# Causal attention inside a four-layer kernel: TensorE makes the products with the values, and the sums of a first half, for two rounds at a time

## The chip, the core and the metric

One NeuronCore of one Trainium2 chip runs the whole program in one launch. The metric is the device time of one execution in microseconds (us). The engines are TensorE (PE, with PEld for its weight loads), VectorE (DVE), ScalarE (ACT), GpSimd (POOL) and SyncE (SP), which here only issues DMAs. Each has its own instruction stream and runs it in order; between streams there are semaphores.

## The reference

Four layers run one after the other, each with a residual and layer norms around it: a convolution model, a feed-forward layer, this attention, and a feed-forward layer with mixed LoRA experts. The change touches the attention alone:

```python
b, t, d = x.shape                       # 2, 1024, 1024; H, G, HD = 32, 8, 32
q = jnp.dot(x, Wq).reshape(b, t, H, HD).transpose(0, 2, 1, 3)
kv = jnp.dot(x, Wkv).reshape(b, t, G, 2, HD).transpose(2, 3, 0, 1, 4)
k, v = (kv[:, 0], kv[:, 1])             # each of the 8 groups is shared by 4 heads
scores = jnp.einsum('bhqd,bhkd->bhqk', q, k)
scores = jnp.where(causal[None, None], -jnp.inf, scores)
weights = jax.nn.softmax(scores * (1.0 / HD ** 0.5), axis=-1)
ctx = jnp.einsum('bhqk,bhkd->bhqd', weights, v)
ctx = ctx.transpose(0, 2, 1, 3).reshape(b, t, d)
return jnp.dot(ctx, Wo) + bo
```

## The kernel before, in words

The program has four stages with a barrier between them. Stage C (`StageC`, lines 1466 to 2222) is the attention; its main loop runs from about 1083 us to 1915 us of the profiled execution.

**Groups.** The loop goes over 16 groups o: two batch entries times eight key groups, each with its four heads g. A group has 48 slots s, and S = 48 o + s counts slots through the whole loop. Slot s is round r = s // 4 of head g = s % 4. A round is one tile of 128 keys against one half (512) of the queries (`ROUNDS`, line 1428): rounds 0 to 3 are the first half, with 512, 384, 256 and 128 queries left by the causal rule, rounds 4 to 11 the second half, with 512 queries in rounds 4 to 8 and then 384, 256 and 128. R = 12 o + r counts rounds through the loop.

**TensorE, per slot** (`pe`, line 1886). It makes the scores of this slot, 128 keys by up to 512 queries (`pe_score`, line 1840), into one of three PSUM banks, which it may reuse once ScalarE has taken the exponential of the slot three before. Then it makes a product for the row maxima of a later group, 60 slots ahead (`pe_amax`, line 1824), into a bank that VectorE must have read (the maxima are taken at lines 2134 and 2138). In slots named by the table `JOBS` it also makes three matmuls of 512 columns of a coming group's queries or keys (`pe_job`, lines 1800 to 1802); 16 such steps are a job of two parts, and `evac_at`, `split_at` and `place_at` say at which slots the results are copied out, the next weights are split into a high and a low part in four pieces, and the results are moved by DMA.

**The products with the values.** Once per round, in its second slot (g == 1), TensorE makes the products of round R - 2 (`pe_pv`, line 1855): four heads, each into its own 32 partitions of bank 5, in the tile shape 128 x 32. The four heads are eight matmul records. In rounds 0 to 3 (and in all of group 15) four more with a matrix of ones follow (`pe_sums`, line 1873), which give the softmax sums of that half. Only after these does the semaphore `pv_s` count the round.

**ScalarE, per slot** (`act`, line 2022). The exponential of the slot goes to the buffer P (`act_exp`, line 2002). P holds three rounds, so the first exponential of round R waits until the products of round R - 3 are counted by `pv_s`; those of the second half also wait for GpSimd's additions from three rounds before. Between the exponentials, in the order of its stream, ScalarE copies out the jobs (line 1966), makes the high parts of the weight pieces (line 1942; in eight groups at slots 18 to 21, behind the exponential of the same slot), and copies out sums and products (lines 2015 and 2020) at slots 6 and 22.

**The sums of the second half.** VectorE adds the exponentials of rounds 4 and 5, one head per slot, after the row maxima of slots 24 to 27 (`dve_pair`, line 2104). GpSimd adds rounds 6 to 11 to that, one after the other (`pool`, line 2219), with the causal masking of the rounds on the diagonal in between (line 2207). In slot 5 of the next group TensorE reduces the result with ones (`pe_sum`, line 1882). GpSimd also multiplies a finished half by its reciprocal sums (line 2197) in rounds 1 and 5.

**Banks.** `tables` (line 1516) plays through the order of the loop and gives each use of three shared banks (3, 4, 6) its bank; the sums of a first half take one at slot 9 and give it back at slot 21.

After group 13 the weights of the next stage (`WO`, line 1463) are loaded and split in pieces too (ScalarE line 1948, VectorE line 2095), at slots of groups 13 to 15; SP issues the next load, and behind it the DMA of the row maxima of the next group, only when VectorE has made the four pieces before.

Of the kernel before, what the change touches and what calls it, by code (L numbers as in the profile page):

```python
# [235 lines left out]
class StageA:  # L236
# [332 lines left out]
    def pe(self, e):  # L569
        e.wait_ge(*self.k.cst_in(2))  # L570
        for name, *at in self.order["pe"]:
            if name[:2] == "b_":
                self.then.first_pe(e, name, *at)
            elif name == "tr":
                self.pe_tr(e, *at)
            elif name == "win":
                self.pe_win(e, *at)
            elif name == "out":
                self.pe_out(e, *at)
            else:  # L580
                self.pe_step(e, name, *at)
# [884 lines left out]
class StageC:  # L1466
# [49 lines left out]
    def tables(self):  # L1516


        self.step_at, self.evac_at, self.place_at, self.split_at = {}, {}, {}, {}
        for n, (what, slots, place) in enumerate(JOBS):  # L1520
            if slots:
                for q, S in enumerate(slots):
                    self.step_at[S] = (n, q)
                self.evac_at[slots[7] + 1], self.evac_at[slots[15] + 1] = (n, 0), (n, 1)
                self.place_at[place[0]], self.place_at[place[1]] = (n, 0), (n, 1)

                soon = n + 1 < len(JOBS) and JOBS[n + 1][1][0] < slots[15] + 8
                for q in range(4):
                    self.split_at.setdefault(slots[15] + 2 + q // (2 if soon else 1), []).append((n + 1, q))
        self.bank_of, self.held_by = {}, {}  # L1530
        given, keeps = [None] * 3, []

        def turn(o, a):
            b = keeps.pop(0)
            self.bank_of[o, a], self.held_by[o, a] = (3, 4, 6)[b], given[b]
            given[b] = o, a
            return b

        keeps += range(3)
        for o, a in [(0, a) for a in range(48)] + [(0, 48)] + [(1, a) for a in range(LEAD)]:  # L1540
            keeps.append(turn(o, a))
        for o in range(16):
            for s in range(48):
                A = 48 * o + s + 48 + LEAD
                if A < 768:
                    keeps.append(turn(A // 48, A % 48))
                if s == 38 and o < 15:
                    keeps.append(turn(o + 1, 48))
                if s == 5 and o > 0:
                    keeps.append(turn(o, 50))  # L1550
                if s == 9:
                    kept = turn(o, 49)
                if s == 21:
                    keeps.append(kept)
        turn(16, 50)
# [330 lines left out]
    def pe(self, e):  # L1886
        for u in range(18):
            if u < 16:
                self.pe_x(e, u)
            if u > 1:  # L1890
                self.pe_v(e, u - 2)
            if u in (10, 11):
                for q in range(8):
                    self.pe_job(e, 0, 8 * (u - 10) + q)
        for n in (1, 2):
            for q in range(16):
                self.pe_job(e, n, q)
        ahead = [(0, a) for a in range(48)] + [(1, a) for a in range(LEAD)]
        for q in range(32):
            self.pe_job(e, 3 + q // 16, q % 16)  # L1900
            for o, a in ahead[max(0, 5 * (q - 8) // 2):max(0, 5 * (q - 7) // 2)]:
                self.pe_amax(e, o, a)
                if a == 47:
                    self.pe_mrow(e, 0)
        for o in range(16):
            for s, (r, g) in enumerate(SLOTS):
                S = 48 * o + s
                self.pe_score(e, o, r, g)
                A = S + 48 + LEAD
                if A < 768:  # L1910
                    self.pe_amax(e, A // 48, A % 48)
                if s == 38 and o < 15:
                    self.pe_mrow(e, o + 1)
                if S in self.step_at:
                    self.pe_job(e, *self.step_at[S])
                if g == 1 and S > 8:
                    self.pe_pv(e, *divmod(S // 4 - 2, 12))
                if s == 5 and o > 0:
                    self.pe_sum(e, o - 1)
        self.pe_pv(e, 15, 10)  # L1920
        self.pe_pv(e, 15, 11)
# [223 lines left out]
    def dve(self, e):  # L2145
        k = self.k
        for u in range(16):
            self.dve_x(e, u)
            if u == 0:
                self.dve_w(e, 0)  # L2150
                self.dve_w(e, 1)
                e.memset(self.maskw[:, 0:384], 0.0).then_inc(self.given_s.s, 1)
            if u in (6, 12):
                self.dve_w(e, 2 if u == 6 else 3)
            if u in (12, 13):
                self.dve_job(e, 0, u - 12)
        e.wait_ge(*self.vmm_s(16))
        e.memset(self.K4[96:97, 0:8:2, :].bitcast(F32), -1.0).then_inc(self.given_s.s, 1)
        e.memset(self.K4[96:97, 1:8:2, :].bitcast(F32), -1.0).then_inc(self.given_s.s, 1)
        e.wait_ge(*self.given_s(3))  # L2160
        for n in (1, 2):
            for part in range(2):
                self.dve_job(e, n, part)
            self.dve_w(e, n + 3)
        ahead = [(0, a) for a in range(48)] + [(1, a) for a in range(LEAD)]
        for q in range(32):
            for o, a in ahead[max(0, 5 * (q - 8) // 2):max(0, 5 * (q - 7) // 2)]:
                self.dve_amax(e, o, a)
            if q % 8 == 7:
                self.dve_job(e, 3 + q // 16, q % 16 // 8)  # L2170
            if q == 15:
                self.dve_w(e, 6)
        for o in range(16):
            for s in range(48):
                S = 48 * o + s
                A = S + 48 + LEAD
                if A < 768:
                    self.dve_amax(e, A // 48, A % 48)
                if S in self.evac_at:
                    self.dve_job(e, *self.evac_at[S])  # L2180
                if 24 <= s < 28 and o < 15:
                    self.dve_pair(e, o, s - 24)
                for n, q in self.split_at.get(S, ()):
                    self.dve_w4(e, n + 1, q)
                for q in range(4):
                    if S - q in WO:
                        self.dve_wo(e, WO.index(S - q), q)
                E = self.finish_at(S, 2)
                if E is not None:
                    self.dve_rec(e, E)  # L2190
        self.dve_rec(e, 31)
# [491 lines left out]
```

## Time and profile before

| | |
|---|---|
| median of 3 runs | 2441.47 us (2439.51 to 2441.91) |
| the profiled execution | 2444.48 us |
| its span, first to last instruction | 2442.8 us |
| busy in the span: PE, DVE, ACT, POOL | 89%, 60%, 38%, 36% |
| mean granted TensorE clock | 0.946 of full speed |

Busy time counts instructions that overlap once, and the end of a matmul is modelled, so a busy TensorE is not one at its peak. The span is shorter than the time of its own execution by 1.68 us. In a row of the time line stand the start (us from the start of the span), the duration, engine, line, operation, the tiles written and read, their shape, how often it is repeated in the row, and in brackets the idle time of the engine before it and what ended that.

### The profile page before, as it was taken

Reading aid. Unit: us, or ns where it says so; the run is one execution under the profiler, and the core shown is the slowest. Engines: PE = TensorE matmul, PEld = TensorE weight load, DVE = VectorE, ACT = ScalarE, POOL = GpSimd, SP = SyncE. Lnnn points to the kernel's source line nnn. Section 1 sums busy time; section 2 is a strip of 40 time slices with the busy share of each in tenths; the row PEclk is TensorE's granted clock in tenths of the full one; section 3 lists DMA queues with packets and bytes.
Section 4 is the critical chain, followed back from the end, with each engine's and each line's share of the span. In section 5 each row is a group of like instructions: output and inputs, shape, how many; then the busy total and the mean of one; then the engine's idle time right before and its main releaser. Section 6 shows DMA issues by size and latency. Waiting matters only on the chain.

```text
span 2442.8 us, 31296 instructions
## 1 busy us (share of the span) xinstructions
PE 2167.2 (89%) x11064; PEld 1530.1 (63%) x11064; DVE 1459.2 (60%) x3261; ACT 924.3 (38%) x1691; POOL 889.7 (36%) x732
## 2 busy tenths in 40 slices
PE   4899965699999969789998899899987699999998
PEld 4655534588888859655555555555543387667676
DVE  7866766577766643277666566676675156543333
ACT  4654633233323223115554455355555222221111
POOL 1344654444444420004664454446654122110000
PEclk9899987899999989889999899999988899999999
DMA  5220445111211227431223622322222555334332
GB/s 164 72 90 1 149 130 193 64 69 71 77 70 70 87 93 267 109 75 45 67 61 85 187 71 68 73 75 67 52 68 65 173 174 172 133 115 158 112 112 95
DMA packets 139572, 249.30 MB, mean 102 GB/s; under 512 B 26885, under 2 KB 69765, under 8 KB 139191
## 3 DMA queue, kind: packets, MB, share of 16 engines
q1 hardware_dynamic: 130711, 230.51, 29.7%
q10 hardware_dynamic: 8704, 16.78, 2.1%
q8 instruction: 88, 1.44, 0.3%
q14 instruction: 69, 0.57, 0.1%
HBM read 139.48 MB, written 76.02 MB: 88 GB/s over the span
## 4 chain that ended last, share of the span: by engine, by line
PE 61%; DVE 11%; POOL 11%; issue 6%; DMA 3%; ACT 3%; SPq 3%; POOLq 0%; DVEq 0%; ACTq 0%
POOL c_S L2219 9%; PE PS L2403 4%; PE PS L2360 4%; PE PS L2361 4%; PE PS L2364 4%; PE PS L1069 3%; PE PS L1070 3%; PE PS L1071 3%; PE PS L1840 3%; PE PS L1824 3%; PE PS L1855 3%; PE PS L1102 2%; DVE PS L2138 2%; PE PS L1800 2%; PE PS L1104 2%
## 5 line engine op out<-in xcount | busy, mean ns | idle before, releaser
L2002 ACT ACTIVATE c_P<-PS 128x512 f32<-128x512 f32 (+3 forms) x768 | 360.6, 495 | 378.4 <-PE PS L1840 359.7
L2219 POOL TENSOR_TENSOR c_S<-c_S,c_P 128x2048 f32<-128x2048 f32 (+1 forms) x90 | 313.7, 3485 | 74.4 <-DVE c_S L2104 67.2
L1824 PE MATMUL PS<-c_K,c_Q 96*128 96x512 f32 (+3 forms) x768 | 283.3, 379 | 54.3 <-DVE cst L2138 27.2
L1840 PE MATMUL PS<-c_Q,c_K 97*128 97x512 f32 (+3 forms) x768 | 283.1, 381 | 9.2 <-DMA c_Q<-c_mT 5.6
L1840 PEld LDWEIGHTS PS<-c_Q,c_K 97*128 97x128 f32 x768 | 149.3, 197 | 169.5 <-ACT c_P L2002 74.1
L2134 DVE TENSOR_REDUCE cst<-PS 128x1 f32<-128x512 f32 x256 | 176.1, 688 | 97.3 <-PE PS L1824 97.0
L1824 PEld LDWEIGHTS PS<-c_K,c_Q 96*128 96x128 f32 x768 | 151.7, 198 | 124.6 <-DVE cst L2138 61.7
L2207 POOL TENSOR_SCALAR_AFFINE_SELECT c_P<-c_P 128x512 f32<-128x512 f32 x128 | 82.4, 644 | 373.1 <-ACT c_P L2002 373.1
L1855 PE MATMUL PS<-c_P,c_V 128*32 128x512 f32 (+3 forms) x1536 | 172.0, 521 | 19.0 <-ACT c_P L2002 11.3
L2138 DVE CUSTOM_DVE_ANT_0 PS<-PS,maskw 128x128 f32<-128x128 f32 (+3 forms) x256 | 126.8, 507 | 87.5 <-PE PS L1824 87.3
L2360 PE MATMUL PS<-c_xth,d_xh 128*128 128x512 f32 x384 | 157.2, 409 | 19.1 <-DVE d_xl L2475 19.1
L2138 DVE CUSTOM_DVE_ANT_0 PS<-PS,maskw,cst 128x128 f32<-128x128 f32 (+3 forms) x256 | 142.4, 556 | 46.9 <-PE PS L1824 31.6
L199 POOL TENSOR_TENSOR maskw<-maskw,mhalf 128x1 f32<-128x1 f32 x64 | 36.6, 572 | 360.3 <-DVE maskw L168 360.3
L1069 PE MATMUL PS<-b_w13h,b_xsh 128*128 128x460 f32 (+1 forms) x384 | 148.3, 386 | 16.6 <-DVE b_xsl L1274 16.3
L1301 DVE SCALAR_TENSOR_TENSOR b_pr<-b_g,b_a 128x460 f32<-128x460 f32 x192 | 158.3, 860 | 1.6
L1193 ACT ACTIVATE b_g<-PS 128x460 f32<-128x460 f32 x96 | 53.0, 554 | 267.5 <-PE PS L1076 267.5
L2361 PE MATMUL PS<-c_xtl,d_xh 128*128 128x512 f32 x384 | 152.4, 397 | 0.0
L1395 POOL TENSOR_TENSOR b_gp<-b_g 128x230 f32<-128x230 f32 x96 | 84.8, 883 | 165.3 <-DVE b_g L1286 165.3
L1070 PE MATMUL PS<-b_w13l,b_xsh 128*128 128x460 f32 (+1 forms) x384 | 143.9, 375 | 0.0
L1071 PE MATMUL PS<-b_w13h,b_xsl 128*128 128x460 f32 (+1 forms) x384 | 143.0, 372 | 0.0
L1800 PE MATMUL PS<-c_xth,c_wh 128*128 128x512 f32 x304 | 126.5, 416 | 8.3 <-DVE c_ql L2123 5.1
L1286 DVE TENSOR_TENSOR b_g<-b_g,PS 128x460 f32<-128x460 f32 x96 | 60.4, 629 | 119.2 <-ACT b_g L1193 119.2
(280 smaller groups left out, 4876.0 us busy)
## 6 DMA issues: line engine op xcount, KB each, us to landing
a_xin<-in_x SPq DMA_DIRECT2D x32, 512.0 KB, 4.3
c_Q<-c_qh SPq DMA_DIRECT2D x256, 64.0 KB, 2.0
d_x<-scr SPq DMA_DIRECT2D x32, 512.0 KB, 3.9
scr<-a_xin SPq DMA_DIRECT2D x16, 512.0 KB, 5.5
scr<-a_hid SPq DMA_DIRECT2D x16, 512.0 KB, 2.9
b_xn<-scr SPq DMA_DIRECT2D x16, 512.0 KB, 5.6
b_x<-scr SPq DMA_DIRECT2D x16, 512.0 KB, 4.8
scr<-b_x SPq DMA_DIRECT2D x16, 512.0 KB, 2.6
```

The costliest lines, as they stand in the source:

```text
L1069: e.matmul(o, self.xsh[:, par, i, :], wh[:, v, i, :], start=i == 0, stop=False)
L1070: e.matmul(o, self.xsh[:, par, i, :], wl[:, v, i, :], start=False, stop=False)
L1071: e.matmul(o, self.xsl[:, par, i, :], wh[:, v, i, :], start=False, stop=False)
L1824: e.matmul(bank[:, 0:hi - lo], self.Q4[0:96, 4 * (o % 3) + g, 128 * t:128 * t + 128], self.K4[0:96, HEADS[o % 8], lo:hi], start=True, stop ...
L1840: e.matmul(self.k.bank(i % 3)[:, 0:hi - lo], self.K4[0:97, HEADS[o % 8], 128 * kt:128 * kt + 128], self.Q4[0:97, 4 * (o % 3) + g, lo:hi], ...
L1855: m = e.matmul(k.bank(5)[32 * g:32 * g + 32, lo - 512 * half:512], self.V[:, kt, o // 8, HEADS[o % 8], :], P[:, g, 0:hi - lo], start=kt == ...
L2002: e.activation(self.P[:, R % 3, g, 0:hi - lo], self.k.bank(i % 3)[:, 0:hi - lo], ACT.Exp, scale=SCALE).then_inc(self.exp_s.s, 1)
L2134: e.tensor_reduce(m, r, AX, ALU.max).then_inc(self.mx_s.s, 1)
L2138: e.tensor_tensor_reduce(out=r, in0=r, in1=self.maskw[:, 512 - n:512], scale=1.0, scalar=m if lo > 0 else -3.0e38, op0=ADD, op1=ALU.max, a ...
L2219: e.tensor_tensor(S[:, :, 512 - n:512], S[:, :, 512 - n:512], P[:, :, 0:n], ADD).then_inc(self.psum_s.s, 1)
L2360: e.matmul(o, h, wh[:, c, cols], start=c == 0, stop=False)
L2361: e.matmul(o, h, wl[:, c, cols], start=False, stop=False)
```

## The change

TensorE makes the products with the values only in every second round, in slots 5, 13, 21, 29, 37 and 45, and there for the two rounds R - 3 and R - 2. The bank of a first half's sums is therefore taken at slot 13 and no longer at slot 9. VectorE's four additions of rounds 4 and 5 move one slot later.

```diff
@@ tables
-                if s == 9:
+                if s == 13:
                     kept = turn(o, 49)
@@ pe
-                if g == 1 and S > 8:
-                    self.pe_pv(e, *divmod(S // 4 - 2, 12))
+                if s % 8 == 5 and S > 8:
+                    for R in (S // 4 - 3, S // 4 - 2):
+                        self.pe_pv(e, *divmod(R, 12))
                 if s == 5 and o > 0:
                     self.pe_sum(e, o - 1)
@@ dve
-                if 24 <= s < 28 and o < 15:
-                    self.dve_pair(e, o, s - 24)
+                if 25 <= s < 29 and o < 15:
+                    self.dve_pair(e, o, s - 25)
```

TensorE, group 12, from the products at slot 17 to the end of those at slot 21. L1840 is a slot's scores, L1824 the product for the maxima, L1855 the products with the values, L1873 the sums. Before:

```order
L1855 MATMUL PS<-c_P,c_V 32x256 x4
L1873 MATMUL PS<-c_P,cst 32x256 x4
L1840 MATMUL PS<-c_Q,c_K 128x512
L1824 MATMUL PS<-c_K,c_Q 128x512
L1840 MATMUL PS<-c_Q,c_K 128x512
L1824 MATMUL PS<-c_K,c_Q 128x256
L1840 MATMUL PS<-c_Q,c_K 128x512
L1824 MATMUL PS<-c_K,c_Q 128x512
L1840 MATMUL PS<-c_Q,c_K 128x512
L1824 MATMUL PS<-c_K,c_Q 128x384
L1855 MATMUL PS<-c_P,c_V 32x128 x4
L1873 MATMUL PS<-c_P,cst 32x128 x4
```

Now, TensorE from slot 18 to the end of the products at slot 21:

```order
L1840 MATMUL PS<-c_Q,c_K 128x512
L1824 MATMUL PS<-c_K,c_Q 128x512
L1840 MATMUL PS<-c_Q,c_K 128x512
L1824 MATMUL PS<-c_K,c_Q 128x256
L1840 MATMUL PS<-c_Q,c_K 128x512
L1824 MATMUL PS<-c_K,c_Q 128x512
L1840 MATMUL PS<-c_Q,c_K 128x512
L1824 MATMUL PS<-c_K,c_Q 128x384
L1855 MATMUL PS<-c_P,c_V 32x256 x4
L1873 MATMUL PS<-c_P,cst 32x256 x4
L1855 MATMUL PS<-c_P,c_V 32x128 x4
L1873 MATMUL PS<-c_P,cst 32x128 x4
```

The products and sums of round 2 (256 columns) moved from slot 17 to slot 21, behind the scores of slots 18 to 21 and in front of those of round 3.

VectorE, group 12, from the maxima of slot 24. `ISA` at L2138 are the masked maxima with their accumulator read, L2104 is the addition of rounds 4 and 5. Before:

```order
L2138 ISA PS,cst<-PS,maskw 128x128
L2138 ISA cst 128x1
L2104 TENSOR_TENSOR c_S<-c_P 128x512
L2138 ISA PS,cst<-PS,maskw 128x256
L2138 ISA cst 128x1
L2104 TENSOR_TENSOR c_S<-c_P 128x512
L2138 ISA PS,cst<-PS,maskw 128x384
L2138 ISA cst 128x1
L2104 TENSOR_TENSOR c_S<-c_P 128x512
L2138 ISA PS,cst<-PS,maskw 128x512
L2138 ISA cst 128x1
L2104 TENSOR_TENSOR c_S<-c_P 128x512
```

Now, from the maxima of slot 25 (every line of this function is one further down):

```order
L2139 ISA PS,cst<-PS,maskw 128x256
L2139 ISA cst 128x1
L2105 TENSOR_TENSOR c_S<-c_P 128x512
L2139 ISA PS,cst<-PS,maskw 128x384
L2139 ISA cst 128x1
L2105 TENSOR_TENSOR c_S<-c_P 128x512
L2139 ISA PS,cst<-PS,maskw 128x512
L2139 ISA cst 128x1
L2105 TENSOR_TENSOR c_S<-c_P 128x512
L2135 TENSOR_REDUCE cst<-PS 128x1
L2105 TENSOR_TENSOR c_S<-c_P 128x512
```

The fourth addition now stands behind one more instruction, the maxima of slot 28 (TENSOR_REDUCE). The streams of ScalarE, GpSimd and SP are as they were.

## Rows read from the trace of the kernel before

**Rows 1.** The page: busy time in the span by engine, share and instructions.

```profile
PE 2167.2 (89%) x11064; PEld 1530.1 (63%) x11064; DVE 1459.2 (60%) x3261; ACT 924.3 (38%) x1691; POOL 889.7 (36%) x732
```

**Rows 2.** Time line, POOL, group 12: multiplication in round 5, additions of rounds 6, 7.

```profile
1741.26 1.27 POOL L2197 TENSOR_TENSOR c_cH<-c_cH,c_cS 128x512 f32<-128x512 f32 x1 [7.56 <-ACT c_P L2002]
1746.46 9.32 POOL L2219 TENSOR_TENSOR c_S<-c_S,c_P 128x2048 f32<-128x2048 f32 x2 [3.93 <-DVE c_S L2104]
```

**Rows 3.** Time line, PE: reductions at slot 5 (groups 5, 12, 13), a wait before.

```profile
1350.93 1.04 PE L1882 MATMUL PS<-c_S,cst 128*32 128x512 f32 x8
...
1721.25 1.07 PE L1882 MATMUL PS<-c_S,cst 128*32 128x512 f32 x8 [0.22 <-POOL c_S L2219]
...
1765.91 0.64 PE L1855 MATMUL PS<-c_P,c_V 128*32 128x256 f32 x8 [1.01 <-ACT c_P L2002]
...
1770.25 1.06 PE L1882 MATMUL PS<-c_S,cst 128*32 128x512 f32 x8 [0.23 <-POOL c_S L2219]
```

**Rows 4.** Time line, PE: products at slot 33 of group 12 and what follows.

```profile
1749.07 1.07 PE L1855 MATMUL PS<-c_P,c_V 128*32 128x512 f32 x8
1750.06 0.50 PE L1840 MATMUL PS<-c_Q,c_K 97*128 97x512 f32 x1
1750.40 0.39 PE L1824 MATMUL PS<-c_K,c_Q 96*128 96x512 f32 x1
1750.64 0.39 PE L1800 MATMUL PS<-c_xth,c_wh 128*128 128x512 f32 x1
```

**Rows 5.** Time line, PE: products and sums at slots 17 and 21 of group 12.

```profile
1734.35 0.64 PE L1855 MATMUL PS<-c_P,c_V 128*32 128x256 f32 x8
1734.80 0.61 PE L1873 MATMUL PS<-c_P,cst 128*32 128x256 f32 x8
...
1737.75 0.45 PE L1824 MATMUL PS<-c_K,c_Q 96*128 96x384 f32 x1 [0.16 <-DVE cst L2138]
1738.13 0.43 PE L1855 MATMUL PS<-c_P,c_V 128*32 128x128 f32 x8
```

**Rows 6.** Time line, ACT, group 12: weight piece of slot 19, exponential of slot 20.

```profile
1737.17 0.41 ACT L1942 CAST c_wh<-c_raw 128x256 fp32r<-128x256 f32 x1
1737.46 0.61 ACT L2002 ACTIVATE c_P<-PS 128x512 f32<-128x512 f32 x1
```

**Rows 7.** Time line, DVE, group 12: low parts, first and last addition of rounds 4, 5.

```profile
1735.50 0.69 DVE L2123 TENSOR_TENSOR c_ql<-PS,c_qh 128x512 fp32r<-128x512 f32 x1 [0.63 <-ACT c_qh L1966]
...
1738.55 0.42 DVE L2090 TENSOR_TENSOR c_wl<-c_raw,c_wh 128x256 fp32r<-128x256 f32 x1
...
1741.51 1.57 DVE L2104 TENSOR_TENSOR c_S<-c_P 128x512 f32<-128x512 f32 x1
1743.00 0.42 DVE L2138 CUSTOM_DVE_ANT_0 PS<-PS,maskw 128x256 f32<-128x256 f32 x1
...
1745.63 0.68 DVE L2104 TENSOR_TENSOR c_S<-c_P 128x512 f32<-128x512 f32 x1
```

**Rows 8.** Time line, DVE, group 14: pieces of slots 27 and 28, maxima between.

```profile
1846.50 0.41 DVE L2095 TENSOR_TENSOR c_xtl<-c_raw,c_xth 128x256 fp32r<-128x256 f32 x1
1846.83 0.68 DVE L2134 TENSOR_REDUCE cst<-PS 128x1 f32<-128x512 f32 x1
1847.43 4.13 DVE L2095 TENSOR_TENSOR c_xtl<-c_raw,c_xth 128x256 fp32r<-128x256 f32 x1
```

**Rows 9.** Time line, PE: waits at slot 41 of group 13, slot 0 of group 15.

```profile
1805.06 1.93 PE L1855 MATMUL PS<-c_P,c_V 128*32 128x512 f32 x8 [2.17 <-POOL c_P L2207]
...
1871.08 1.22 PE L1840 MATMUL PS<-c_Q,c_K 97*128 97x512 f32 x2 [5.57 <-DMA c_Q<-c_mT]
```

**Rows 10.** Time line, PE, group 15: from one round's products to the next.

```profile
1897.76 1.06 PE L1855 MATMUL PS<-c_P,c_V 128*32 128x512 f32 x8
...
1899.61 0.96 PE L1840 MATMUL PS<-c_Q,c_K 97*128 97x512 f32 x3
...
1901.22 1.07 PE L1855 MATMUL PS<-c_P,c_V 128*32 128x512 f32 x8
```

## The prediction

> **What bounds the kernel now.** I read the page first: TensorE is busy for 89% of the span [rows 1]. That alone would make it the bound, so the next question is what TensorE waits for in the attention loop. The time line of its reduction at slot 5 answers that. From group 12 to group 13 these lie 1770.25 - 1721.25 = 49.0 us apart, and each is preceded by a wait that GpSimd's last addition ends [rows 3]. I found the same mark, with the same 49.0 us where two such groups follow each other, in ten of the fifteen reductions. Where it is missing (the reduction at 1350.93 has no wait [rows 3]) the groups carry denser jobs, or are the last ones.
>
> So ten groups run in a closed loop of two halves. The first: VectorE ends the fourth addition of rounds 4 and 5, GpSimd starts its own at 1746.46 [rows 2] and TensorE reduces their sum at 1770.25, 23.8 us later. The second: from the reduction at 1721.25 to GpSimd's start at 1746.46, 25.2 us. In the first half TensorE has time to spare: it waits 1.01 us at slot 49 alone [rows 3]. Only what shortens the second half can shorten such a group. The chain of waits for group 12 says what that half is made of: TensorE from slot 5 to slot 17, then ScalarE's copy of the job, and from 1735.50 [rows 7] on VectorE without a gap to the last addition, which starts at 1745.63 [rows 7].
>
> **What the change removes on TensorE.** Eight matmul records of 512 columns between full-width ones take 1750.06 - 1749.07 = 0.99 us. Eight of 256 take 0.45 when more of their own shape follow [rows 5], so 512 would take 0.90: leaving the shape costs 0.09. The scores behind take 0.34 to the next start where 0.24 is usual [rows 4]: 0.10 more. Entering the shape I put at 0.10 too, an estimate by symmetry. That is 0.3 us per visit; 192 rounds made 191 visits and now make 96, so 95 x 0.3 = 28 us of TensorE's time go. In the ten closed groups none of the visits saved in slots 29 to 53 counts: TensorE would only wait longer for GpSimd.
>
> **The second half of a closed group, step by step** (times of group 12).
> 1. Up to slot 17 one visit is saved (rounds 0 and 1 share slot 13), and a little of TensorE's waiting: 0.4 us. VectorE's low part of the job starts at about 1735.1, not 1735.5 [rows 7].
> 2. The products of round 2 leave slot 17 for slot 21. There TensorE needs the bank of the maxima of slot 19 (two banks are free while the sums hold the third). It got it at 1737.75, after a wait for VectorE [rows 5]; now at about 1737.3. From that product to the start of the group was 0.38, and products and sums of round 2 take 1734.80 + 0.61 - 1734.35 = 1.06 [rows 5]: done at about 1738.7.
> 3. The exponential of slot 20 is the first of round 5 and needs the buffer of round 2. It ran at 1737.46 [rows 6]; now it can't before 1738.8. ScalarE's weight piece of slot 20 stands behind it in the same stream, and is done about 0.9 later, at 1739.7. VectorE's low part of that piece, which ran at 1738.55 [rows 7], now starts at 1739.7, and VectorE, ready at 1738.1, stands idle for 1.6 us in the middle of the half that bounds the loop. All behind it is 1.1 us later.
> 4. The first addition took 1.57 us instead of 0.68 because GpSimd's multiplication, 1741.26 to 1742.53 [rows 2], held it: the next instruction came at 1743.00 [rows 7]. The multiplication waits for round 5 too, so it moves to about 1742.5 to 1743.8. VectorE gets to the first addition at 1741.51 + 1.1 + 0.35 (the maxima of slot 25 are now ahead of it) = 1743.0, and is held again until 1743.8. Its successor starts at 1744.2, 1.2 later than before.
> 5. From there to the last addition it was 1745.63 - 1743.00 = 2.63 [rows 7]. In this stretch the maxima of slot 25 (0.35) are replaced by those of slot 28, 0.60 from start to start [rows 8]: 2.9. The last addition starts at 1747.1, **1.5 us later**.
>
> Bounds for this: 0.2 a group if step 3's gap doesn't open (step 1 and the extra maxima then nearly cancel), 2.2 if TensorE gets to slot 21 late by the 0.7 that the products of a 384-wide round take. I take 1.5, since every link of it is a row. Eight groups (1, 2, 3, 6, 7, 10, 11, 12) have weight pieces at slots 18 to 21: 8 x 1.5 = **+12.0**. Group 9 has them at slots 20 to 23: **+1.0**. Groups 0 and 13 have none; there only the maxima (0.6) against the saved visit (0.3) count: **+0.6** for both.
>
> **Groups 4, 5 and 9**, where TensorE doesn't wait at slot 5, gain what it saves: six visits each, 3 x 6 x 0.3 = 5.4. Part of it will meet transfers and low parts of jobs that VectorE makes late, so I take **-4.0** (0 to -7; low parts that fall into a GpSimd addition can move either way).
>
> **Group 14.** VectorE's weight piece of slot 28 ran for 4.13 us, because GpSimd had just started its addition; the piece of slot 27, which came before that start, took 0.41 [rows 8]. Now the last addition and the piece both stand in slot 28, directly one behind the other, so the piece starts at once. By the Trainium skill (SBUF — State Buffer, "SBUF: two separate sides") whichever of the two engines starts first holds the shared port pair for its whole instruction; by that rule the piece would pass, and the trace agrees with both its sides. The pieces of slots 36 to 39 then end one GpSimd addition earlier (9.32 / 2 = 4.7 [rows 2]), and with them the 5.57 us wait for the maxima's DMA [rows 9] shrinks. GpSimd's start itself is 0.9 later (maxima 0.6, piece 0.3). **-3.8** (0 to -5).
>
> **Group 15.** No maxima are left; a round takes 1901.22 - 1897.76 = 3.46 us, 1.85 of it products and sums [rows 10]. In pairs: 2 x 1.85 - 0.2, then 1.61 and four exponentials at 0.5 through three banks, 7.1 against 6.9. Three pairs at full width: **+0.6**.
>
> **The sum:** 12.0 + 1.0 + 0.6 - 4.0 - 3.8 + 0.6 = **+6.4 us**. The profiled execution took 2444.48 us, which would become 2450.9; the median of the runs lies 3.0 below it, so I predict **2448 us**. 0.2%, about what a measurement of this kernel can tell from no change, is 4.9 us.
>
> **Rivals.**
> - *The gap in step 3 doesn't open* (chance 0.20). If VectorE frees the banks of slots 18 and 19 earlier than I think, round 2 is counted before ScalarE needs it. For it speaks that the pieces are small; against it that TensorE was already waiting for VectorE in slot 21. The point from which it decides: the exponential of slot 20 no more than 0.6 behind the piece of slot 19. Then 8 x 0.2 replaces 12 and 0.2 the 1.0 of group 9, and the sum is -4.8: 2437 us.
> - *TensorE is the bound after all* (0.03): all 28 us come off, 2413 us. The Trainium skill (Perfetto Trace Analysis, "Identifying the Most-Contended Engine") says to optimize the engine with the highest occupancy first, though it warns that TensorE's busy share misleads; by the plain rule this rival is the forecast. The 49.0 us loop speaks against it.
> - *The gains elsewhere cancel the loss* (0.22): same terms, but groups 4, 5, 9 and 14 at their lower bounds (-7 and -5) or a closed group at 0.9: -1 to +4, about 2443 us.
> - *The clock falls* (0.12). TensorE now reaches slot 45 earlier and waits there longer for GpSimd's masking of round 9: the 1.01 of slot 49 and the time saved add up to some 1.6. After a wait of 2.17 the same eight matmuls took 1.93 instead of 1.06 [rows 9], so the clock was at 1.2 GHz and not at 2.4. After 1.01 they were not slowed. If 1.6 is enough, each closed group pays about 1.2 more past its slack: +6 + 10 x 1.2, 2460 us.
> - *The change doesn't do what it says*: in the second half round 9's products still wait for their masking, so a pair is split by a wait. It only matters where TensorE bounds, and is in the range.
>
> **How the numbers follow.** My forecast has 0.43 and reaches from +5 to +12 (2446 to 2454), since the terms 12, -4 and -3.8 carry 2 to 4 us each. With the clock rival the other side is slower too: 0.55. The first rival lies on the bound of 4.9: 0.12 of it is faster, 0.08 no change. With the third rival that makes 0.30 within 0.2%, and with the second 0.15 faster. The range of 8 in 10 leaves out the 28 us gain and the far end of the clock rival: 2434 to 2458.
>
> **What would show it.** In a closed group: the exponential of slot 20 starting at once behind round 2's sums, more than 1 us after the weight piece of slot 19; an idle of 1 to 2 us on VectorE before a low part of a weight piece; the first addition again at some 1.5 us; reductions at slot 5 some 50.5 us apart, still ended by GpSimd, and TensorE's waits before them longer by the visits saved. In group 14 no piece of 4 us at slot 28. It is wrong if the reductions lie 49 us apart or less, or if GpSimd no longer ends TensorE's wait at slot 5.

## The result, and the profile after

The changed kernel took 2464.99 us (median of 4 runs, 2461.43 to 2468.1), the kernel before beside it on the same chip 2440.49 (4 runs, 2439.33 to 2441.91). The ratio is 1.0096, with a 95% interval of 1.0081 to 1.011: **24.5 us slower**. The forecast was 2448 us, with a range from 2434 to 2458. The direction was right, the size was not.

The profiled execution took 2466.18 us, its span was 2464.5. The engines' line of its page [rows 1]:

```profile
PE 2171.0 (88%) x11064; PEld 1546.2 (63%) x11064; DVE 1453.7 (59%) x3261; ACT 913.8 (37%) x1691; POOL 889.2 (36%) x732
```

The same instructions and hardly more busy time on TensorE (2171.0 us against 2167.2), yet 21.7 us more span. In the attention loop, from the first scores to the last products, it is 849.7 us against 830.1: 19.6 us. The rest lies ahead of the loop (1.7) and behind it (0.4), where the program is unchanged. TensorE's mean granted clock over the loop was 0.95 of full speed before and is 0.92 now.

Below, a *closed group* is one of the eight groups 1, 2, 3, 6, 7, 10, 11 and 12, for which the prediction had 1.5 us each. A *first half* runs from the reduction at slot 5 to GpSimd's first addition (it is what the prediction calls the second half, the one that it expects to grow), a *second half* from there to the next reduction.

**A closed group in which the clock stayed up.** Group 12, TensorE: reduction, slots 20 and 21, then the products of round 9 in the next half and the next reduction [rows 3, 5].

```profile
1740.09 1.06 PE L1882 MATMUL PS<-c_S,cst 128*32 128x512 f32 x8 [0.84 <-POOL c_S L2220]
...
1753.53 0.39 PE L1840 MATMUL PS<-c_Q,c_K 97*128 97x512 f32 x1
1755.22 0.50 PE L1824 MATMUL PS<-c_K,c_Q 96*128 96x512 f32 x1 [1.30 <-DVE cst L2135]
...
1756.39 0.64 PE L1855 MATMUL PS<-c_P,c_V 128*32 128x256 f32 x8
1756.84 0.61 PE L1873 MATMUL PS<-c_P,cst 128*32 128x256 f32 x8
1757.28 0.40 PE L1855 MATMUL PS<-c_P,c_V 128*32 128x128 f32 x8
...
1782.15 0.85 PE L1855 MATMUL PS<-c_P,c_V 128*32 128x384 f32 x8 [1.57 <-ACT c_P L2003]
...
1790.63 1.06 PE L1882 MATMUL PS<-c_S,cst 128*32 128x512 f32 x8 [0.84 <-POOL c_S L2220]
```

ScalarE there: weight piece of slot 19, exponential of slot 20, weight piece of slot 20 [rows 6].

```profile
1755.00 0.42 ACT L1943 CAST c_wh<-c_raw 128x256 fp32r<-128x256 f32 x1
1757.59 0.60 ACT L2003 ACTIVATE c_P<-PS 128x512 f32<-128x512 f32 x1 [2.16 <-PE PS L1873]
1758.08 0.40 ACT L1943 CAST c_wh<-c_raw 128x256 fp32r<-128x256 f32 x1
```

VectorE: low part of that piece, first and last addition [rows 7]; and GpSimd's multiplication and first addition [rows 2].

```profile
1758.51 0.43 DVE L2091 TENSOR_TENSOR c_wl<-c_raw,c_wh 128x256 fp32r<-128x256 f32 x1 [1.67 <-ACT c_wh L1943]
...
1761.86 1.33 DVE L2105 TENSOR_TENSOR c_S<-c_P 128x512 f32<-128x512 f32 x1
...
1766.00 0.68 DVE L2105 TENSOR_TENSOR c_S<-c_P 128x512 f32<-128x512 f32 x1
```

```profile
1761.36 1.27 POOL L2198 TENSOR_TENSOR c_cH<-c_cH,c_cS 128x512 f32<-128x512 f32 x1 [9.29 <-ACT c_P L2003]
1766.82 9.34 POOL L2220 TENSOR_TENSOR c_S<-c_S,c_P 128x2048 f32<-128x2048 f32 x2 [4.18 <-DVE c_S L2105]
```

Counted in us from the reduction, the exponential of slot 20 now starts at 17.50 (before 16.21), the low part of its piece at 18.42 after an idle of 1.67, and GpSimd's addition at 26.73 (before 25.21). That is the forecast chain, link by link: +1.52 us, and 50.54 us from one reduction to the next. TensorE's wait of 1.30 us at slot 20 (row 1755.22) is not in the forecast. In the kernel before it was 0.20 there:

```profile
1736.87 0.50 PE L1824 MATMUL PS<-c_K,c_Q 96*128 96x512 f32 x1 [0.20 <-DVE cst L2134]
```

**A closed group in which the clock fell.** The same place in group 2:

```profile
1204.04 0.50 PE L1824 MATMUL PS<-c_K,c_Q 96*128 96x512 f32 x1 [1.29 <-DVE cst L2135]
...
1205.29 1.08 PE L1855 MATMUL PS<-c_P,c_V 128*32 128x256 f32 x8
1206.15 1.08 PE L1873 MATMUL PS<-c_P,cst 128*32 128x256 f32 x8
1207.00 0.66 PE L1855 MATMUL PS<-c_P,c_V 128*32 128x128 f32 x8
```

The windows over these products, and over the 5.8 us of work up to the wait:

```profile
core 0: us, PE busy (x), PEclk, DMA share, GB/s
1205.23:1208.13 2.90, 2.90 (x34) 0.50 0.12 40
1196.93:1202.73 5.80, 5.80 (x39) 1.00 0.02 1
```

The granted clock was 1.00 (2.4 GHz) ahead of the wait and 0.50 (1.2 GHz) behind it, and the first half took 27.68 us, 2.44 more than before. The clock fell like this in groups 1, 2, 3 and 10 of this trace; groups 6, 7, 8, 11, 12 and 13 have the same 1.3 us wait at slot 20 and kept the fast clock.

**The last groups.** Group 14, VectorE, the last addition and the piece of slot 28 [rows 8], and the wait for the maxima's DMA in group 15 on TensorE [rows 9]:

```profile
1869.01 0.68 DVE L2105 TENSOR_TENSOR c_S<-c_P 128x512 f32<-128x512 f32 x1
1869.61 0.42 DVE L2096 TENSOR_TENSOR c_xtl<-c_raw,c_xth 128x256 fp32r<-128x256 f32 x1
```

```profile
1889.59 3.75 PE L1840 MATMUL PS<-c_Q,c_K 97*128 97x512 f32 x6 [1.99 <-DMA c_Q<-c_mT]
```

The piece takes 0.42 and not 4.13, and the wait 1.99 and not 5.57, as forecast.

### The profile page after: what moved, and what is told of

It is laid out like the page before. It is cut to its first block and busy times, and to the rows that moved or that the text cites. A ratio compares the mean times of both kernels' runs of the same rounds, so it can differ in the third digit from the quotient of the medians.

```text
span 2464.5 us, 31296 instructions
## 1 busy us (share of the span) xinstructions
PE 2171.0 (88%) x11064; PEld 1546.2 (63%) x11064; DVE 1453.7 (59%) x3261; ACT 913.8 (37%) x1691; POOL 889.2 (36%) x732
## 5 line engine op out<-in xcount | busy, mean ns | idle before, releaser
L2003 ACT ACTIVATE c_P<-PS 128x512 f32<-128x512 f32 (+3 forms) x768 | 352.0, 497 | 424.7 <-PE PS L1840 149.3
L1824 PE MATMUL PS<-c_K,c_Q 96*128 96x512 f32 (+3 forms) x768 | 284.1, 381 | 68.0 <-DVE cst L2139 30.1
L1840 PE MATMUL PS<-c_Q,c_K 97*128 97x512 f32 (+3 forms) x768 | 283.0, 381 | 16.0 <-ACT c_P L2003 13.4
L1824 PEld LDWEIGHTS PS<-c_K,c_Q 96*128 96x128 f32 x768 | 153.5, 200 | 132.5 <-DVE cst L2139 55.4
L1840 PEld LDWEIGHTS PS<-c_Q,c_K 97*128 97x128 f32 x768 | 151.5, 198 | 123.8 <-ACT c_P L2003 87.9
L1855 PE MATMUL PS<-c_P,c_V 128*32 128x512 f32 (+3 forms) x1536 | 174.4, 553 | 10.5 <-POOL c_P L2208 8.9
```

The lines of the kernel that those rows point to most:

```text
L1824: e.matmul(bank[:, 0:hi - lo], self.Q4[0:96, 4 * (o % 3) + g, 128 * t:128 * t + 128], self.K4[0:96, HEADS[o % 8], lo:hi], start=True, stop ...
L1840: e.matmul(self.k.bank(i % 3)[:, 0:hi - lo], self.K4[0:97, HEADS[o % 8], 128 * kt:128 * kt + 128], self.Q4[0:97, 4 * (o % 3) + g, lo:hi], ...
L1855: m = e.matmul(k.bank(5)[32 * g:32 * g + 32, lo - 512 * half:512], self.V[:, kt, o // 8, HEADS[o % 8], :], P[:, g, 0:hi - lo], start=kt == ...
L2003: e.activation(self.P[:, R % 3, g, 0:hi - lo], self.k.bank(i % 3)[:, 0:hi - lo], ACT.Exp, scale=SCALE).then_inc(self.exp_s.s, 1)
```

## The experiments

Eleven kernels ran in three sittings, one chip each. Each was timed beside the kernel before on that chip, and its ratio is to those times. A trace is of one execution, which is not always near the median. The theory in its first form (A) was the prediction's: late products, held exponential, held weight piece, VectorE idle, and a clock that falls on top of it.

### Weight pieces out of the way

```diff
@@ tables, in the changed kernel
-                    self.split_at.setdefault(slots[15] + 2 + q // (2 if soon else 1), []).append((n + 1, q))
+                    self.split_at.setdefault(slots[15] + 2 + q // 2, []).append((n + 1, q))
```

> The changed kernel, with the weight pieces of slots 18 to 21 made at 18, 18, 19, 19, so none stands in ScalarE's stream behind the exponential of slot 20. Theory A (the late products of round 2 hold that exponential, the piece behind it and so VectorE, and the wait that this gives TensorE lets its clock fall in some groups): VectorE's gap before the piece of slot 20 goes, the way from the reduction at slot 5 to GpSimd's first addition falls from 26.7 (27.7 in groups 1, 2, 3, 10) to about 25.5 us, TensorE's 1.3 us wait at slot 20 is gone and its clock doesn't fall there: about 2465 - 8 x 1.2 - 4 x 1.0 = 2451 us (2446 to 2456). Theory B (it is the later place of VectorE's additions, with the maxima of slot 28 in front of the last): 2463 us or more. Theory C (the clock falls for another reason): the 1.2 come off but groups 1, 2, 3, 10 stay a microsecond longer than the others, 2455 us.

Measured 2463.57 us, ratio 1.0082 (1.0069 to 1.0094). As a forecast of the time a miss, 12 us off. The trace says why: VectorE's gap behind a held piece is gone, but TensorE's 1.3 us wait at slot 20 is not. Group 2 kept the clock, group 7 did not:

```profile
1206.94 0.50 PE L1824 MATMUL PS<-c_K,c_Q 96*128 96x512 f32 x1 [1.29 <-DVE cst L2135]
...
1208.44 0.64 PE L1855 MATMUL PS<-c_P,c_V 128*32 128x256 f32 x8
...
1482.49 0.50 PE L1824 MATMUL PS<-c_K,c_Q 96*128 96x512 f32 x1 [1.29 <-DVE cst L2135]
...
1484.23 1.08 PE L1855 MATMUL PS<-c_P,c_V 128*32 128x256 f32 x8
```

With the clock up (groups 2, 6, 12) a first half was 0.65 to 0.71 us longer than before, with the clock down up to 2.38. It fell in 6 of the 10 groups with that wait, against 4 of 10 in the changed kernel's trace. The late pieces are thus about 0.8 of the 1.5 us. Theory A's second half was wrong: I had the origin of the wait wrong: it isn't made by VectorE's gap, which comes after it. It stands where the products of round 2 used to fill TensorE's time while VectorE made the low part of the job and the maxima of slot 18.

### Only rounds 2 and 3 together

```diff
@@ pe, in the kernel before
-                if g == 1 and S > 8:
-                    self.pe_pv(e, *divmod(S // 4 - 2, 12))
+                if g == 1 and S > 8 and s != 17:
+                    for R in range(S // 4 - (3 if s == 21 else 2), S // 4 - 1):
+                        self.pe_pv(e, *divmod(R, 12))
```

> The kernel before, with one visit of each group moved: the products and sums of round 2 leave slot 17 and stand at slot 21 ahead of those of round 3. All other rounds keep their own visit, and the additions their slots. Theory A: the gap of VectorE opens as in the changed kernel, without the extra maxima: 8 x (0.9 to 1.2) and some 4 us for the clock, so 2440 + 12 = 2452 us (2446 to 2456). Theory B: nothing but one saved visit of 0.3 us a group, 2438 to 2441 us.

2466.79 us, 1.0094 (1.0081 to 1.0106): above theory A's range, and as large a loss as the changed kernel's (1.0096) from one moved visit. (The trace is of its fastest execution, 2459.64 us.) In the only closed group whose clock stayed up (group 7) the first half was 1.74 us longer; in the other seven 2.21 to 2.84. ScalarE and VectorE in group 7 show the forecast gap:

```profile
1476.85 0.60 ACT L2003 ACTIVATE c_P<-PS 128x512 f32<-128x512 f32 x1 [2.15 <-PE PS L1873]
```

```profile
1477.77 0.43 DVE L2091 TENSOR_TENSOR c_wl<-c_raw,c_wh 128x256 fp32r<-128x256 f32 x1 [1.66 <-ACT c_wh L1943]
```

### All but rounds 2 and 3

```diff
@@ pe, in the changed kernel
-                if s % 8 == 5 and S > 8:
-                    for R in (S // 4 - 3, S // 4 - 2):
+                if (s % 8 == 5 or s == 17) and S > 8:
+                    for R in range(S // 4 - (2 if s in (17, 21) else 3), S // 4 - 1):
```

> The changed kernel, with rounds 2 and 3 back at slots 17 and 21, one visit each. All other rounds are in pairs and the additions one slot later. Theory A: no gap at slot 20, only the maxima (0.6) against one visit (0.3) in the closed half, gains in groups 4, 5, 8, 9 and 14: about 2438 us (2434 to 2443). Theory B: the loss stays, 2455 us or more. A third view, that any pair costs (the first exponential of rounds 7, 9 and 11 is held too): between them, with GpSimd's additions starting later.

2439.39 us, 0.9986 (0.9975 to 0.9997), as theory A expected. Its 12 executions lie far apart, 2431.92 to 2446.93 us, and the trace is of the fastest. The eight closed first halves were 0.20 to 0.26 us shorter than before, and TensorE's wait at slot 20 was 0.20 again:

```profile
1725.64 0.50 PE L1824 MATMUL PS<-c_K,c_Q 96*128 96x512 f32 x1 [0.20 <-DVE cst L2135]
```

So pairs as such don't cost a closed first half anything; this pair does.

### Pairs two slots earlier

```diff
@@ pe, in the changed kernel (the bank of the sums is taken at slot 11, additions in slots 24 to 27)
-                if s % 8 == 5 and S > 8:
-                    for R in (S // 4 - 3, S // 4 - 2):
+                if s % 8 == 3 and S > 8:
+                    for R in (S // 4 - 2, S // 4 - 1):
```

> Pairs as in the changed kernel, but in slots 3, 11, 19, 27, 35 and 43, for the rounds R - 2 and R - 1, so that each pair is counted before the next exponential needs its buffer; the additions are back in slots 24 to 27, the bank of the sums is taken at slot 11. Theory A: no exponential waits for products, a closed half from the reduction to GpSimd's start is 24.7 us against 25.2 before: 2436 us (2430 to 2441). Rival D (what costs is the pair itself, two rounds of products in a row through which TensorE makes no scores, or the masks of round 9 that are now wanted two slots earlier): over 2450 us, with TensorE waits of 2 us and more at slot 43 and its clock at half after them.

2450.99 us, 1.0042 (1.0026 to 1.0058). Half a hit: the closed first halves were 0.70 to 0.75 us shorter, as theory A said, but five of the eight second halves were 2.0 to 2.9 us longer, as rival D said. TensorE wants the masked round 9 in slot 43 before GpSimd has it, in twelve groups (1.48 to 2.90 us); group 11's row:

```profile
1716.15 0.85 PE L1855 MATMUL PS<-c_P,c_V 128*32 128x384 f32 x8 [2.52 <-POOL c_P L2208]
```

### Early pairs ahead of the masks, late ones behind

```diff
@@ pe, in the kernel of the last experiment
-                if s % 8 == 3 and S > 8:
-                    for R in (S // 4 - 2, S // 4 - 1):
+                if S > 8 and s in (5, 11, 19, 27, 35, 45):
+                    for R in (S // 4 - 3, S // 4 - 2) if s in (5, 45) else (S // 4 - 2, S // 4 - 1):
```

> Pairs in slots 11, 19, 27 and 35 for the rounds R - 2 and R - 1, where each is counted before the next exponential needs its buffer, but in slots 45 and 5 for R - 3 and R - 2 as in the changed kernel, so that rounds 8 to 11 get the time that GpSimd's masks take. Additions in slots 24 to 27. Theory now: in the run with slots 3 to 43 the closed half from the reduction to GpSimd's start was 0.7 us shorter and the other half 2 us longer, since the mask of round 9 was late by 2.5 us at slot 43. Here the 2.5 us wait goes and the other half is back at 23.8 us: 2442 - 13 x 0.6 - 5 = 2430 us (2426 to 2436). Rival (two rounds of products in a row cost in the second half too): 2440 us or more, second halves above 24.5 us.

2432.61 us, 0.9962 (0.9949 to 0.9974), within the expected range: faster than the kernel before. The closed first halves are 0.70 to 0.75 us shorter, their second halves as before (group 3's 0.5 shorter). Group 8, which is not closed, gained 2.6 in its first half and lost 2.3 in its second. Group 12, TensorE's pair at slot 19 and ScalarE's exponential of slot 20:

```profile
1724.74 0.64 PE L1855 MATMUL PS<-c_P,c_V 128*32 128x256 f32 x8
...
1725.85 0.40 PE L1873 MATMUL PS<-c_P,cst 128*32 128x128 f32 x8
```

```profile
1726.72 0.60 ACT L2003 ACTIVATE c_P<-PS 128x512 f32<-128x512 f32 x1 [0.16 <-PE PS L1840]
```

The exponential waits for its scores, no longer for products, and starts 15.5 us after the reduction.

### Work in place of the wait

```diff
@@ pe_score, in the changed kernel
-        e.matmul(self.k.bank(i % 3)[:, 0:hi - lo], self.K4[0:97, HEADS[o % 8], 128 * kt:128 * kt + 128],
-                 self.Q4[0:97, 4 * (o % 3) + g, lo:hi], start=True, stop=True).then_inc(self.score_s.s, 1)
+        for n in range(6 if 4 * r + g == 20 and o < 15 else 1):
+            m = e.matmul(self.k.bank(i % 3)[:, 0:hi - lo], self.K4[0:97, HEADS[o % 8], 128 * kt:128 * kt + 128],
+                         self.Q4[0:97, 4 * (o % 3) + g, lo:hi], start=True, stop=True)
+        m.then_inc(self.score_s.s, 1)
```

> The changed kernel, but the scores of slot 20 are made six times over into the same bank in groups 0 to 14, so that TensorE works 1.15 us in place of most of its 1.3 us wait for VectorE there. Theory (the wait lets the clock fall to 1.2 GHz in some groups, and the products of rounds 2 and 3 then take 3.4 us and not 2.1): the clock stays up at slot 21 in every group, all closed halves are 26.7 us, and the time is 5 x 1.0 lower, 2460 us (2457 to 2462), although TensorE does more. Rival (the clock falls for what TensorE has done over a longer stretch): still 27.7 us in some groups, 2465 us or more.

2462.48 us, 1.0081 (1.0067 to 1.0095), at the upper end of the expected range. In group 2 (1204.04 above), TensorE now reads:

```profile
1199.83 1.55 PE L1841 MATMUL PS<-c_Q,c_K 97*128 97x512 f32 x6
1201.52 0.50 PE L1824 MATMUL PS<-c_K,c_Q 96*128 96x512 f32 x1
...
1202.68 0.64 PE L1857 MATMUL PS<-c_P,c_V 128*32 128x256 f32 x8
1203.14 0.61 PE L1875 MATMUL PS<-c_P,cst 128*32 128x256 f32 x8
```

```profile
core 0: us, PE busy (x), PEclk, DMA share, GB/s
1202.70:1204.90 2.20, 2.20 (x36) 1.00 0.13 46
```

The clock stayed up at slot 21 in all ten such groups, and all eight closed first halves were 1.48 to 1.53 us longer than before: five more matmuls in each group cost these halves nothing and give the clock back. The 3.8 us that the eight gained did not reach the whole. The loop took 850.6 us in this trace against 850.3 in the changed kernel's, and the interval of the ratio overlaps with that kernel's (1.0081 to 1.011), so a shorter time is not shown. Group 3's second half was 2.6 us longer than before (in the changed kernel as long as before), group 6's 1.2, group 5's first half 2.0 and group 9's 1.3. In groups 3 and 6 the clock fell at another place. In group 3 TensorE waited for VectorE for 2.51 us at slot 36, VectorE for 3.75 us for the DMA of the softmax sums (`sum_d`), and the 4.4 us of work behind had a mean clock of 0.61.

### Additions back in slots 24 to 27

```diff
@@ dve, in the changed kernel
-                if 25 <= s < 29 and o < 15:
-                    self.dve_pair(e, o, s - 25)
+                if 24 <= s < 28 and o < 15:
+                    self.dve_pair(e, o, s - 24)
```

> The changed kernel with VectorE's additions back in slots 24 to 27. Theory: the maxima of slot 28 (0.6) no longer stand before the last addition, those of slot 25 are again behind the first; 0.3 to 0.6 us a closed half: 2465 - 12 x 0.45 = 2460 us (2456 to 2463). Group 14 gets its 4 us piece at slot 28 back, which costs up to 4 of this. Rival: all the difference of the closed half: 2450 us.

2464.62 us, 1.009 (1.0076 to 1.0104): nothing gained, outside my range. The closed first halves were 1.23 to 1.71 longer than before, 1.23 to 1.37 in all but one, so the maxima of slot 28 cost 0.25 and not 0.45. Against this gain, group 14's second half was 4.2 us longer than in the changed kernel, and group 3's 2.1.

### Both: pieces early, wait filled

The edits of the first and sixth experiment together.

> Both edits: the weight pieces at slots 18, 18, 19, 19 and the scores of slot 20 six times over. Theory: without the clock and without the late pieces the closed half has only the late exponential, the extra maxima and the saved visit left, 25.9 us (25.24 + 0.65, as in the one closed half of the run with early pieces in which the clock stayed up): 2442 + 8 x 0.7 + 4 = 2452 us (2448 to 2456). Rival: the fill is paid in full, 1.1 us a group, 2463 us or more.

2448.05 us, 1.0022 (1.0013 to 1.0032), at the lower end of the range. Seven of the eight closed first halves were 0.67 to 0.73 longer than before, group 3's 1.26. With the pieces early, the same five matmuls a group made the kernel 15 us faster (1.0082 to 1.0022, with intervals that don't touch). Not all of that is the clock at slot 21. The eight closed first halves gave 5.9 us between the two traces, and group 5 alone 4 us, for which the part on groups 4, 5 and 8 below has another reason.

### The best form

```diff
@@ pe, in the kernel with pairs in slots 11, 19, 27, 35, 45 and 5
-                if S > 8 and s in (5, 11, 19, 27, 35, 45):
+                if 8 < S < 729 and s in (5, 11, 19, 27, 35, 45):
...
+                if g == 1 and S >= 729:
+                    self.pe_pv(e, *divmod(S // 4 - 2, 12))
@@ dve
-                if 24 <= s < 28 and o < 15:
-                    self.dve_pair(e, o, s - 24)
+                if 24 + (o > 12) <= s < 28 + (o > 12) and o < 15:
+                    self.dve_pair(e, o, s - 24 - (o > 12))
```

> The kernel with pairs in slots 11, 19, 27, 35, 45 and 5, and two edits for the last groups: VectorE's additions one slot later in groups 13 and 14 only, where the weight piece of slot 28 otherwise runs into GpSimd's addition, and one visit per round in group 15. Theory: group 14's second half is again 4 us shorter, as in all runs with the additions in slots 25 to 28, and the last group 1 to 2 us: 2433 - 5 = 2428 us (2425 to 2432). Rival: the 4 us are given back behind it, in the chain of weight loads: 2432 us or more.

2428.05 us, 0.9942 (0.9927 to 0.9957), the fastest of all: 12.8 us under the kernel before. Group 14's second half is 4.1 us shorter than in the kernel before (0.3 without the two edits), and from the last reduction to the last products it is 34.3 us against 39.2 without the two edits. The mean granted clock over that stretch was 0.97 against 0.88, so not all of it is the work saved.

### Single visits in group 15

```diff
@@ pe, in the changed kernel
-                if s % 8 == 5 and S > 8:
+                if s % 8 == 5 and 8 < S < 729:
...
+                if g == 1 and S >= 729:
+                    self.pe_pv(e, *divmod(S // 4 - 2, 12))
```

> The changed kernel, but from slot 9 of group 15 on one visit per round. Theory (in group 15 every exponential of an even round waits for a pair, 2.5 us against the 0.6 forecast): 2465 - 2 = 2463 us, and from the reduction of group 15 to the loop's end 39 us and not 41.3. Rival: the 2.5 us came from the maxima's DMA and the clock in that group: no change, 2465 us.

2460.28 us, 1.0073 (1.0059 to 1.0087). From the last reduction to the last products 35.8 us, where the changed kernel takes 40.6 (two of its waits for exponentials there are 0.78 us each). That is 4.8 us, more than I expected, but it is not the price of the pairs alone: the mean granted clock over the stretch was 0.91 here and 0.83 in the changed kernel. By an estimate from the windows to the end of the last products (41.25 us in the changed kernel, 36.44 here), 0.17 x 41.25 - 0.09 x 36.44 = 3.7 us more of full-speed clock were missing in the changed kernel, which may be the greater part of the 4.8. Up to group 14 this kernel is the changed one instruction by instruction, and yet the clock at slot 21 fell in six of its ten groups (1, 2, 3, 10, 11, 12). Group 12, which kept it in the changed kernel's trace:

```profile
1752.24 0.50 PE L1824 MATMUL PS<-c_K,c_Q 96*128 96x512 f32 x1 [1.30 <-DVE cst L2137]
...
1753.66 1.08 PE L1855 MATMUL PS<-c_P,c_V 128*32 128x256 f32 x8
```

### The additions alone

The diff's second part (additions in slots 25 to 28), in the kernel before.

> The kernel before, with only VectorE's additions one slot later (25 to 28). Theory from the runs with all visits in pairs (a closed half of 26.5 with the additions at 24, of 26.75 at 25): +0.25 in 12 closed halves, -4 in group 14 with up to 2.5 given back behind it: 2443 us (2439 to 2446). Rival: 0.6 in every closed half and no gain in group 14: 2450 us.

2443.61 us, 1.0004 (0.9993 to 1.0016), as expected. The closed first halves are 0.21 to 0.28 longer; group 14's second half is 4.6 shorter and the last reduction to the last products 3.8 (34.3 against 38.1). Here too the clock has a part: 0.96 of full speed over the stretch against 0.87 before, by the same estimate 0.13 x 38.73 - 0.04 x 34.96 = 3.6 us. TensorE's wait for the DMA of the maxima ahead of it was 1.99 us in place of 5.57.

## Why the prediction was right in its direction and wrong in its size

**Which step failed.** The path through a closed group was right. What failed are three terms of the sum. The clock was put at nothing, and TensorE's new wait at slot 20, behind which it fell, was not seen: 3.8 us in the closed first halves, and 2.2 more in the second half of group 10. The gain of the dense groups was put at -4.0, and groups 4, 5 and 8 gave -0.7. Groups 14 and 15 were put at -3.2 together and came out at +0.2.

**What bounds the kernel: right.** Half of the reductions' period is GpSimd's 23.8 us, the other a chain through TensorE, ScalarE and VectorE. The visits saved, 28 us by the estimate, on the engine that is busy for 88% bought nothing there. One sign of being wrong came in part: GpSimd still ends TensorE's wait at slot 5 in six of the ten reductions, but in groups 1, 2, 3 and 11 TensorE now comes later than GpSimd, by 0.2 us at most in three of them and by 2.2 in group 11, behind the fallen clock of group 10.

The Trainium skill (Perfetto Trace Analysis, "Identifying the Most-Contended Engine") says to optimize the engine with the highest occupancy first, and warns that for TensorE this share is a bad measure. By the plain rule the forecast would have been a gain; the measured time, 24.5 us longer, disagrees.

**Steps 1 to 5: right.** The low part of the piece of slot 20 came 18.42 us after the reduction (forecast 1739.7 - 1721.25 = 18.45), VectorE stood idle for 1.67 (1.6), GpSimd's multiplication held the first addition for 1.33, and the half was 1.52 longer (1.5). The runs give the pieces of it, with the clock up: rounds 2 and 3 together +1.74 (second experiment), the other visits saved -0.23 - 0.25 = -0.48 (third, less the additions), the additions' new slots +0.25 (last); 1.74 - 0.48 + 0.25 = 1.51. Of the 1.74, 0.8 is the piece behind the held exponential (the first and eighth experiment). One inner price was off: I put the first rival, no gap for VectorE, at 0.2 a half. It is 0.7, since the exponentials of round 5 are late by themselves, and GpSimd's multiplication with them: in group 2 of the first experiment they start 17.8 and 21.0 us after the reduction, where before it was 16.2 and 20.0 (group 12).

**The clock: the mechanism was named as a rival, at the wrong place, and left out of the sum.** I looked for a longer wait at slot 45. That came (1.57 us in group 12; the row names ScalarE, but GpSimd's mask of round 9 ran from 1781.36 to 1782.00, just up to its end), and the products behind it took 0.85 as ever. The wait that mattered is one that I had read past: in step 2, I moved round 2's 1.06 us of work behind slot 20's maxima and kept TensorE's time for them, and did not write down that TensorE then has nothing to do there. It waits 1.3 us for VectorE, and behind that wait the clock is at 1.2 GHz in some groups: 4 of 10 in the changed kernel's trace, and 6, 7, 5 and 6 of 10 in the other four that keep the wait (early pieces, only rounds 2 and 3, additions at 24, single visits in 15). Together that is 28 of 50; with the wait filled, 0 of 20. A fallen clock costs a first half 0.9 us more (2.44 against 1.52). That the wait is a cause is shown by the filled wait. Why the clock stays up behind the same wait in other groups is open. The rival's 2460 us come nearest to the measured time by luck: its price, 1.2 us in ten groups at slot 45, was not what was paid.

**The sum, term by term** (us against the kernel before, from the two profiled executions):

| stretch | forecast | measured |
|---|---|---|
| first halves of the eight closed groups | +12.0 | +15.9 (12.1 with the wait filled, 3.8 of clock) |
| group 9 | +1.0 | +0.4 |
| first halves of groups 0 and 13 | +0.6 | +1.5 |
| groups 4 and 5 (forecast with part of 9), and 8, which had no term | -4.0 | -0.7 |
| second half of group 10 | 0 | +2.2 |
| second half of 13, group 14 | -3.8 | -2.3 |
| from the last reduction to the last products of group 15 | +0.6 | +2.5 |
| other second halves | 0 | +0.2 |
| loop | +6.4 | +19.6 (terms 19.7) |

- Groups 0, 13 and 8 have no pieces behind the exponential of slot 20, and I took that for no loss. With only rounds 2 and 3 together, group 13's first half was 0.6 us longer and group 8's 0.7: the held exponential alone costs that. (Group 0's was 2.1 shorter in that trace, and with the additions alone 0.7 longer; what places it was not followed.)
- The gains of the dense groups weren't there. Group 4 gained 2.0, group 8 lost 0.8, and group 5 lost 0.5. With rounds 2 and 3 apart, group 8 gained 0.7 and group 5 4.6. Group 5's first half lay anywhere from 5.0 us shorter to 2.0 longer over these kernels, with TensorE's clock at half in parts of it and a wait for VectorE at slot 19 of 0.7 to 7.8 us. VectorE itself waits there for the DMA that brings the sums of group 4's second half. Its idle time was 1.7 and 1.0 us in the two traces in which the half took 28.2 and 29.7 us (the third and the eighth experiment), and 3.6 to 8.0 us in the other eleven, with 31.5 to 35.2 us. So group 5's large differences go with the arrival of a DMA. What delays it was not tried, and what part of group 5's gain is owed to the edits is open. The rows of the changed kernel and of the third experiment:

```profile
1379.19 0.25 DVE L2144 RECIPROCAL cst<-cst 128x16 f32<-128x16 f32 x1 [4.14 <-DMA cst<-sum_d]
...
1363.30 0.25 DVE L2144 RECIPROCAL cst<-cst 128x16 f32<-128x16 f32 x1 [1.71 <-DMA cst<-sum_d]
```

- Group 10's second half: its pair in slot 37 took 3.64 us, where the same pair of group 12 took 1.92. The clock again (0.50 over the 3.64 us), behind a wait of 2.37 us at slot 36 for VectorE, which had itself stood idle for 3.12 us until the DMA of the sums landed:

```profile
1668.67 0.25 DVE L2144 RECIPROCAL cst<-cst 128x16 f32<-128x16 f32 x1 [3.12 <-DMA cst<-sum_d]
...
1669.62 0.45 PE L1824 MATMUL PS<-c_K,c_Q 96*128 96x128 f32 x1 [2.37 <-DVE cst L2139]
...
1671.91 3.64 PE L1855 MATMUL PS<-c_P,c_V 128*32 128x512 f32 x16
```

- Group 14: the term's mechanism is confirmed by the piece of 0.42 us, the DMA wait of 1.99 and the run with the additions alone (-4.6). Its first half was 4.1 longer instead of 0.9. The mean clock over it was 0.88 against 0.95 before, by an estimate 0.12 x 28.70 - 0.05 x 24.61 = 2.2 of these; the rest is open.
- Group 15: "7.1 against 6.9" for two rounds, from the even pace of single visits. The tenth experiment has 4.8 us for the pairs, and the eleventh -3.8 for the additions, both with the clock in them, as said there. I had neither: the two nearly hid each other.

The remaining 2.8 us: the median of before lies 4.0 under its profiled execution, that of the changed kernel 1.2 under its own. I had taken 3.0 for both.

## What to carry to other kernels

Before work is moved on an engine, write down what it fills where it stands. Here it filled a wait for another engine at no cost, and where it went it stood on the path. Two rounds of work can share a visit if the visit comes before the next user of the buffer and after the last producer; each direction has its own limit (here slot 19 was early enough for the exponentials and 21 was not; slot 45 was late enough for the masks and 43 was not), and the pattern need not be the same all through. And a loss that a saved item "should" outweigh is found fastest by making half of the change: one moved visit in a group cost as much as the whole change.

## What the runs showed of the hardware

I had not expected that the clock would fall behind a wait of only 1.3 us, nor that this would differ between groups and executions of the same instructions (groups 11 and 12: up in the changed kernel's trace, down in that of the tenth experiment). Work that computes nothing new can buy it back: five repeated matmuls of 0.23 us each in a 1.3 us wait kept the products and sums behind them at 2.4 GHz in 20 groups of 20. That alone did not clearly shorten the kernel (1.0081 against 1.0096, with intervals that overlap); together with the early weight pieces it went from 1.0082 to 1.0022.
